# Counting edges in node blocks of 128 instead of 125, with degrees kept in that layout

## The reference

```python
dout = jnp.maximum(segment_sum(ones, src), 1.0) ** (-0.5)
din  = jnp.maximum(segment_sum(ones, dst), 1.0) ** (-0.5)

def _gcn_conv(x, src, dst, dout, din, W, b):
    m = (x * dout[:, None])[src]
    agg = jax.ops.segment_sum(m, dst, num_segments=N)
    return agg * din[:, None] @ W + b

h = _gcn_conv(x, src, dst, dout, din, W1, b1)
h = _gcn_conv(h, src, dst, dout, din, W2, b2)
x = _layernorm(x + h)
x = _layernorm(x + message_network(x, node_vec1, src, dst, edge_attr_4, edge_attr_64, ...))
```

## Time and profile before

| | us |
|---|---|
| median of 3 runs | 11765.43 |
| lowest, highest | 11762.11, 11776.07 |
| profiled execution | 11772.34 |
| its span in the trace | 11770.4 |
| counting stage, 282 to 2106 | 1824 |
| first convolution, 2143 to 3840 | 1697 |
| second convolution, 3920 to 5560 | 1640 |
| from 5740 on | 6030 |

### The profile page before, as it was taken

How to read it: one execution, slowest core, us unless ns; L and a number is a source line. 1 busy time by engine, 2 the same in 40 slices (tenths; PEclk the granted TensorE clock), 3 DMA queues, 4 the chain that set the end, 5 groups by cost and what they waited for, 6 DMA issues and landing times. The chain is left out here.

```text
span 11770.4 us, 144439 instructions
## 1 busy us (share of the span) xinstructions
PE 9065.9 (77%) x46003; PEld 5541.3 (47%) x46004; DVE 4978.5 (42%) x12579; ACT 3058.9 (26%) x5769; POOL 3607.9 (31%) x3535
## 2 busy tenths in 40 slices
PE   1999999699999799999566666666666666666665
PEld 1444444244444344444455555555555555555554
DVE  3999999300000200000545444444444544444446
ACT  0999999200000100000322121111121212121113
POOL 6000000000000100000455555555555555555553
PEclk9999999799999899999778787787777878888787
DMA  1444444555555555555422222222222222222222
GB/s 27 170 179 179 176 176 176 171 201 204 202 202 199 159 201 204 202 202 175 125 57 57 56 53 53 54 57 54 55 54 58 55 56 56 56 56 57 54 58 80
DMA packets 578210, 1372.93 MB, mean 117 GB/s; under 512 B 198805, under 2 KB 337012, under 8 KB 571528
## 3 DMA queue, kind: packets, MB, share of 16 engines
q1 hardware_dynamic: 455938, 1144.76, 28.0%
q0 software_dynamic: 109440, 217.84, 7.3%
q10 hardware_dynamic: 12550, 6.40, 0.2%
HBM read 1010.19 MB, written 358.46 MB: 116 GB/s over the span
## 5 line engine op out<-in xcount | busy, mean ns | idle before, releaser
L1454 POOL DMA_INDIRECT t_rows<-table,t_ends x3224 | 3297.3, 1023 | 2580.7 <-issue 1556.9
L917 PE MATMUL c_sums<-c_a,c_parts 125*128 125x500 bf16 x15000 | 3211.8, 375 | 133.4 <-DVE c_parts L902 133.4
L917 PEld LDWEIGHTS c_sums<-c_a,c_parts 125*128 125x128 bf16 x15000 | 1444.3, 96 | 1900.4 <-DVE c_parts L902 142.6
L642 ACT ACTIVATE a_a_sb<-a_sums 128x1000 bf16<-128x1000 f32 x1250 | 1653.6, 1323 | 181.3 <-PE a_sums L625 27.6
L966 POOL DMA_INDIRECT r_rows<-table,r_ends x16 | 15.9, 993 | 5214.3 <-DMA r_ends<-in_edges 5210.0
L1558 PE MATMUL t_sums<-t_hot,t_msg_bc 128*128 x8000 | 1131.0, 287 | 513.5 <-issue 511.4
L1555 PEld LDWEIGHTS t_sums<-t_hot,t_msg_ad 128*128 128x128 f32 x8000 | 1154.0, 225 | 554.2 <-issue 553.3
L1555 PE MATMUL t_sums<-t_hot,t_msg_ad 128*128 x8000 | 1187.1, 310 | 231.8 <-DVE t_hot L1643 169.8
L1522 PE MATMUL t_layer<-t_scal_t,c_w_fc 128*128 128x512 f32 x806 | 551.0, 773 | 1039.6 <-issue 680.0
L600 DVE TENSOR_SCALAR a_key_hot<-a_key_tab,key_t 128x500 bf16<-128x500 f16 x5000 | 1350.3, 345 | 0.0
L973 DVE MEMSET degree_rest<- 128x99 f32 x2 | 0.3, 141 | 3063.7 <-PEq L839 3063.7
(11 more groups left out here) (215 smaller groups left out, 5886.5 us busy)
## 6 DMA issues: line engine op xcount, KB each, us to landing
c_a<-a_dram SPq DMA_DIRECT2D x500, 1250.0 KB, 5.5
a_dram<-a_a_sb SPq DMA_DIRECT2D x50, 6250.0 KB, 17.2
t_scal<-in_edge_attr SPq DMA_DIRECT2D x403, 256.0 KB
t_rows<-table,t_ends POOLq DMA_INDIRECT x3224
t_ends<-in_edges SPq DMA_DIRECT2D x403, 8.0 KB
t_attrs<-in_edge_attr SPq DMA_DIRECT2D x403, 16.0 KB
c_x<-in_x SPq DMA_DIRECT2D x10, 625.0 KB
table<-c_x ACTq DMA_DIRECT2D x10, 625.0 KB
```

Of the source, the lines that this page charges most:

```text
L642: act.activation(a_sb[:, b % 2, :, at * 2 * WIN:(at + 1) * 2 * WIN].rearrange("p h (w d) -> p w h d", w=2), sums[:, side:side + 2, 0:WCOLS ...
L917: mm = pe.matmul(sums[s % 2][:], parts[:, k, i * HCH + h], a_sb[0:LO, n % ASLOTS, :, h], start=i == 0 and h == 0 and k == 0, stop=i == NHC ...
L1454: pool.indirect_dma_start(out=rows[:, slot, t, :], out_offset=None, in_=table, in_offset=bass.IndirectOffsetOnAxis(ap=ends[:, slot, t:t + ...
```

## The change

LO becomes 128 and HI = 98: a source is `hi` = source >> 7 and `lo` = source & 127, the same blocks of 128 nodes that the node stages use. So WCOLS, the columns of a window, go from 500 to 490, and the span from 300 to 294 matmuls. In detail:

- In find_windows VectorE takes a group apart before it is turned (shift, mask, two subtractions, a cast, an add), and ScalarE writes `lo_pair` and `key_t` right from PSUM. The in-degrees are summed there from a comparison of 1280 columns, stored to DRAM in runs of 5 numbers, and the check of the total is made.
- In count_edges the eviction runs over [hi, window, destination] instead of [window, hi, destination], and the two degree matmuls of a pair each take half of hi with ten destinations, instead of all hi with five. The read-back rows and count_degrees are gone.
- source_degrees and norm_degrees become one block ahead of the first convolution, which counts both ends of the leftover group.
- convolve_counts works in 14 chunks of 7 source blocks from 128 partitions, with four buffers of x instead of two and six of A instead of four; VectorE scales the next chunk before it splits the current one. The last chunk has six whole blocks and one of 84 rows.
- convolve_rest no longer counts degrees.

```diff
-LO = 125
-HI = N // LO
+HI = NB
...
-HCH = 10
+HCH = 7
 NHC = HI // HCH
-ASLOTS = 4
+XSLOTS = 4
+ASLOTS = 6
...
@@ find_windows, VectorE @@
+                    dve.tensor_scalar(by_row(hi_i), src, 7, None, ALU.arith_shift_right)
+                    dve.tensor_scalar(by_row(lo_i), src, P - 1, None, ALU.bitwise_and).then_inc(chain, 1)
+                    dve.tensor_scalar(by_row(rel), dst, own[:, j:j + 1], None, ALU.subtract)
+                    dve.tensor_scalar(by_row(rel_hi), dst, own[:, j:j + 1], float(HI), ALU.subtract, ALU.mult
+                                      ).then_inc(taken, 1)
...
+                    dve.tensor_copy(lo[:, b], lo_i[:, b]).then_inc(chain, 1)
...
+                    dve.tensor_tensor(key[:, b], rel_hi[:, b], hi_i[:, b], ALU.add).then_inc(split, 1)
+                    dve.tensor_tensor(hit[:, b], rel[:, b, None, :].to_broadcast([P, WIN, EW]), column[:], ALU.is_equal
                                       ).then_inc(chain, 1)
...
+                    dve.tensor_reduce(degree[:, j, :], hit[:, b], AX.X, ALU.add).then_inc(degree_ready, 1)
...
@@ find_windows, SyncE @@
+                sp.wait_ge(degree_ready, WG)
+                sp.dma_start(degree_dram.rearrange("(j p d) -> p j d", p=P, d=WIN), degree[:]).then_inc(stored, 16)
...
@@ count_edges, TensorE and ScalarE @@
                     for i in range(2):
-                        to = (at * 2 + i) * WIN
-                        mm = pe.matmul(over_d[:, 0:WCOLS], ident[:], a_sb[:, b % 2, :, to:to + WIN],
-                                       start=n == 0 and i == 0, stop=n == NW // 2 - 1 and i == 1)
+                        mm = pe.matmul(over_d[:, i, 0:HALF * both], ident[:],
+                                       a_sb[:, b % 2, i * HALF:(i + 1) * HALF, at * both:(at + 1) * both],
+                                       start=n == 0, stop=n == NW // 2 - 1)
...
-                        a_sb[:, b % 2, :, at * 2 * WIN:(at + 1) * 2 * WIN].rearrange("p h (w d) -> p w h d", w=2),
-                        sums[:, side:side + 2, 0:WCOLS].rearrange("p w (h d) -> p w h d", h=HI),
+                        a_sb[:, b % 2, :, at * both:(at + 1) * both].rearrange("p h (w d) -> p h w d", w=2),
+                        sums[:, side:side + 2, 0:WCOLS].rearrange("p w (h d) -> p h w d", h=HI),
...
@@ norm_degrees @@
+                sp.dma_start(rows[:], degree_dram[0:NB * P].rearrange("(b p) -> b p", p=P)).then_inc(landed, 16)
...
+                    for k in range(2):
+                        for t in range(T):
+                            mm = pe.matmul(counts[:, k, 0:HI], hot_lo[:, k, t, :], hot_hi[:, k, t, :], start=t == 0,
+                                           stop=t == T - 1)
...
@@ convolve_counts @@
-        x = sb("x", [LO, 2, HCH, D])
-        rest = sb("rest", [LO, 2, HCH, D])
...
-        parts = sb("parts", [LO, 3, HI, D], BF16)
+        x = sb("x", [P, XSLOTS, HCH, D])
+        rest = sb("rest", [P, 2, HCH, D])
+        parts = sb("parts", [P, 3, HI, D], BF16)
...
-                    if i >= 2:
-                        sp.wait_ge(parts_ready, i - 1)
+                    slot = i % XSLOTS
+                    if i >= XSLOTS:
+                        sp.wait_ge(parts_ready, i - (XSLOTS - 1))
...
+                scale(0)
+                for i in range(NHC):
+                    if i + 1 < NHC:
+                        scale(i + 1)
+                    if i >= 2:
+                        dve.wait_ge(parts_ready, i - 1)
+                    take_rest(i)
+                    take_last(i)
...
-                                mm = pe.matmul(sums[s % 2][:], parts[:, k, i * HCH + h], a_sb[0:LO, n % ASLOTS, :, h],
+                                mm = pe.matmul(sums[s % 2][:], parts[:, k, i * HCH + h], a_sb[:, n % ASLOTS, :, h],
...
@@ convolve_rest @@
-                        for t in range(T):
-                            mm = pe.matmul(counts[:, 0:1], hot[:, t, :], c.one_row[:], start=t == 0, stop=t == T - 1)
```

## The result

The changed kernel takes 11443.8 us (median of four, 11414.7 to 11455.0) where the kernel before took 11763.8 (median of four, 11736.1 to 11776.1): a ratio of 0.9727, 95% interval 0.9702 to 0.9753. The profiled execution took 11438.9 us with a span of 11436.7. The forecast was 11428, with a range of 11370 to 11600. It held as a total; the way to it was partly another one.

| step | before | after | change | forecast |
|---|---|---|---|---|
| staging | 282.0 | 292.3 | +10 | -9 |
| counting | 1824 | 1668 | -156 | -140 |
| degrees and norms | 37 | 35.4 | -1.5 | +1 |
| first span, convolution 1 | 173.5 | 85.1 | -88 | -80 |
| 24 spans, convolution 1 | 1522.8 | 1491.8 | -31 | -30 |

The account below looks back on a forecast made before the run. TensorE was taken to bound counting and the steady spans, the DMA queues the first spans. Counting -140, columns -60, first spans -119 and small stages -18 sum to -337 us: median 11428, range 11370 to 11600.

Parts of the forecast that it names:

- The columns: Steady spans of both convolutions: 294 matmuls a span, 62.20 us, 1.27 less in each of 48 spans, -60 us.
- Counting: Counting stage: period per pair of windows falls from 1.457 to 1.345 us, TensorE's 1.332 the largest floor, -140 us.
- rival C: Counting stage: 20-byte runs are free, VectorE's 1.315 us a pair is the bound, -37 us to 11391; chance 0.12.
- The first spans: First span of each convolution: 94 us instead of 174, and 79 instead of 118, together -119 us.
- The even spread: First spans' loads: DMA engines share the work evenly, 6.1 us a chunk in convolution 1, 5.0 in convolution 2.
- Staging: Staging of edges: VectorE's group stays under eight gathers' 10 us; stage end -8 (bounds -14 and +4), cleared table -1.
- The small stages: Staging, degree, norm and rest stages: small savings and costs, in sum -18 us.

Follow-up runs that it names:

- the first experiment: Changed kernel with the eviction's loops back in their old order (writes in runs of 5 numbers): eviction 1299 ns, counting stage 1667.2 us.

## Why the prediction held, point by point

**The columns** came as forecast: 62.16 us a span (62.20). A number of matmuls times a duration from the same trace, on an engine that is busy all the time, leaves little room for error.

**Counting** was -156 instead of -140. All three floors were mis-sized. The eviction: I took 1.30 us, nearest to the only row of this kind, and it was 1.00. The reason given (one side's pattern gets better as the other's gets worse) failed, since the read side has no such price; the first experiment shows it. TensorE: I took 0.25 for a degree matmul, 0.22 was measured, near the bound of 0.208. What set the pace was VectorE at 1.33, where the prediction had 1.315, in the main because it scaled the comparison by its columns although half of its price is fixed. Then TensorE at 1.28 and VectorE at 1.33 met with no loss worth naming (1.334), where I had added 0.013 for an uneven meeting. So rival C's mechanism came true, at 1.334 rather than 1.315. That my forecast of 1.345 was close is in part luck: it put TensorE (1.332) and not VectorE as the bound. Its sum also took 1.457 for the pace of before, where 1824/1250 is 1.459; that is worth 2 us.

**The first spans** were -88 and -43 instead of -80 and -39. The even spread was right: undoing it in the new kernel brings the old times back, and making it in the old one takes 96 us off. In the working, slots appear only as "with four x slots instead of two", without a price; once the spread is there and VectorE looks ahead by a chunk, they are worth 37 and 32 us. In the first convolution chunks came every 4.8 us in the main, where the forecast had 6.1: the DMA engines ran at a share of 1.02, 351 GB/s, better than the sum of the scaled old loads. In the second, TensorE was busy for 64.56 of the 64.60 us from its first matmul on, so there the DMA queues no longer set the pace: it is the bound of 62 that the prediction gave for TensorE, at a granted clock of 0.97, and not the 5.0 a chunk. Against that stands a later first chunk: 12.3 and 10.9 us after the barrier, not 9 and 8.

**Staging** was +10 instead of -9, the one term with the wrong sign, and outside its bounds of -14 to +4. The step that failed is "VectorE's steps per group grow from about 3.5 to 6 us and stay under the 10 us". The steps did; the waits between them didn't, and I had counted none. The trace of before did show them, on VectorE in the same stage, early and late:

```profile
109.72 0.29 DVE L496 TENSOR_SCALAR w_shifted<-w_part 128x256 f32<-128x256 f32 x1
...
248.25 0.29 DVE L496 TENSOR_SCALAR w_shifted<-w_part 128x256 f32<-128x256 f32 x1 [5.99 <-remote]
249.65 0.33 DVE L498 TENSOR_SCALAR w_hi<-w_shifted 128x256 f32<-128x256 f32 x1 [1.11 <-issue]
251.05 1.29 DVE L501 SCALAR_TENSOR_TENSOR lo_pair<-w_hi,w_turned_sb 128x256 bf16<-128x256 f32 x2 [1.06 <-DVE w_hi L498]
...
259.45 0.32 DVE L496 TENSOR_SCALAR w_shifted<-w_part 128x256 f32<-128x256 f32 x1 [5.99 <-remote]
```

The same step waits for nothing in the first groups and 6 us in the late ones, which are 11.2 us apart (16 steps of 0.70) where the gathers need 10. I read how long the instructions take, and put the 18 us behind the last cast down to work; most of it was such waits. Both kernels have three waits a group on VectorE's own results, here 5.99, 1.11 and 1.06 us. Their number is not what changed but their beginning: in the kernel before the first groups have none and they set in after 160 us, in the changed kernel the first group at 75 us has them. So VectorE was 11.2 us a group late from the start, and ended at 285 instead of 282; the store of the in-degrees, which I had named as the unknown, adds its 7 us behind that. On a chip with prompt signals the step holds (275.0).

**The small stages** otherwise came within 3 us in sum. The +18 behind the second convolution can't be told from the spread: from the end of the last span on, the same code took 6216 to 6268 us in the four runs of the first experiments, which shared one chip, and 6224 here.

So the total is nearer to the forecast (-334 against -337) than its parts are. The counting and the first spans gave 28 us more than said, staging took 19 back, and 18 came from the messages, within their spread. That these cancel to 3 us is luck.

## What to carry to other kernels

Before the cost of a strided pattern is scaled, ask which side pays it and whether the length of the run matters: here 10-byte runs cost 30% over 20-byte runs on both engines, in TensorE's reads (0.295 against 0.225 us) and ScalarE's writes (1.299 against 0.998), and 20-byte runs next to nothing (0.225 against 0.208 for a contiguous sum matmul; 0.998 against an estimated 1.02 for a plain eviction). Half of the price of a 490-column key comparison on VectorE is fixed (0.13 of 0.259 us, by the estimate above), so fewer and longer instructions gained 25 us in the counting stage, where 2% fewer columns gained next to nothing. And the number of partitions in a transfer is a tuning size of its own: cutting 125 into 112 and 13 took 96 us from the two first spans of the old kernel for a few changed lines. Where slots are few, look at the order of the waits too: with two slots VectorE waited for the next chunk before it freed the current one, and loads of 3.9 us and passes of 4.3 us followed each other, 8.2 us a chunk.

## What the runs showed that I had not expected

- In the staging stage, beside GpSimd's gathers, a wait for a semaphore costs VectorE mostly 1.1 to 6.0 us on all chips but one, also when its condition has been met for 5 us, and up to 12 us where it waits for TensorE (the kernel without in-degrees). On that one the same code has none of it. The starts behind these waits lie on a grid of 0.70 us, and the waits end in every such run between 276 and 282 us, some 20 us after the last gather was issued. Where VectorE has just waited 6 us or more for a gather, the waits on its own results behind that are short in most cases (without in-degrees, 19 such waits of 6.7 to 9.1 us, and none over 0.9 us on its own results). I don't know the cause; no run here tells it.
- A load of 50 KB behind a store of 6 MB lands 14 us after its issue through the same queue and through another one, with the DMA engines at a share of 0.93.
- GpSimd's comparison of 128 columns takes 0.61 us and lengthens VectorE's comparisons beside it by 18% (2.56 us for eight instead of 2.17).
